# A LayerNorm, sparse-attention and FP8-linear kernel: the banded product as four 32-row strips, with b2, the quantised x and the order of four engines redone

## The reference

```
xn  = layernorm(x)                                   # x: 4096 rows x 1024, f32
A   = (w1 @ w2.T) * sparse_mask                      # 1024 x 1024, non-zero near the diagonal only
y   = gelu(xn @ A + b2)
xq  = fp8_e5m2(xn * x_scale), x_scale = 57344 / max|xn| over all rows
wq  = fp8_e4m3(weight * w_scale)
out = x + y + (xq @ wq.T) / x_scale / w_scale + bias
```

## Time and profile before

| | us |
|---|---|
| median of 3 runs (293.49 to 294.21) | 294.0 |
| the profiled execution | 293.77 |
| its span, first to last instruction | 292.0 |
| PE busy | 251.1 (86%) |
| DVE busy | 208.8 (72%) |
| POOL busy | 205.7 (70%) |
| ACT busy | 203.0 (70%) |

### The profile page before, as it was taken

One profiled execution on the slowest core, in us unless ns is written; L12 is line 12 of the kernel. 1 busy time (PEld: TensorE's weight loads), 2 busy tenths in 40 slices (PEclk: granted clock), 3 DMA queues, 4 the chain that ended last, 5 costly groups with the idle time before them and its releaser, 6 DMA issues.

```text
span 292.0 us, 4911 instructions
## 1 busy us (share of the span) xinstructions
PE 251.1 (86%) x1818; PEld 175.2 (60%) x1818; DVE 208.8 (72%) x225; ACT 203.0 (70%) x239; POOL 205.7 (70%) x137
## 2 busy tenths in 40 slices
PE   0039699990279799999999999999999999999994
PEld 0039688880278366666666656666666666666661
DVE  3888999999997457956659575567746766656563
ACT  1079979999996698676676749667588687772210
POOL 2000499999997189996978786887789897776333
PEclk9999999997559999999999999999999999999999
DMA  6999999999999239999999999999999989879913
GB/s 235 415 411 410 409 407 410 407 384 408 313 226 142 45 69 198 227 216 224 220 216 229 232 192 251 224 226 215 216 240 209 215 222 214 213 203 225 202 72 147
DMA packets 99721, 72.56 MB, mean 249 GB/s; under 512 B 85488, under 2 KB 87280, under 8 KB 99696
## 3 DMA queue, kind: packets, MB, share of 16 engines
q1 hardware_dynamic: 99696, 72.24, 91.2%
HBM read 34.60 MB, written 16.78 MB: 176 GB/s over the span
## 4 chain that ended last, share of the span: by engine, by line
PE 43%; DMA 21%; ACT 10%; SPq 8%; POOL 7%; issue 6%; DVE 4%; ACTq 0%; POOLq 0%; DVEq 0%
PE psF L1054 12%; PE psT L1054 11%; DMA x_all<-in_L_attn_x_dram 8%; PE psY L1037 8%; PE psZ L1037 8%; DMA home<-home 8%; DMA x_all<-in_L_attn_w_dram 4%; POOL x_all L532 3%; SPq L362 3%; POOL home L494 2%; ACT squares L567 2%; PE psT L970 2%; ACT xq L670 2%; PE psY L980 2%; ACT junk L554 2%
## 5 line engine op out<-in xcount | busy, mean ns | idle before, releaser
L532 POOL TENSOR_TENSOR x_all<-x_all,biases 128x1024 f32<-128x1024 f32 x32 | 75.5, 2361 | 35.0 <-DVE x_all L894 35.0
L494 POOL TENSOR_TENSOR home<-home 128x1024 f16<-128x1024 f32 x32 | 68.3, 2133 | 8.6 <-ACT home L663 8.0
L1054 PE MATMUL psT<-wqT,wq_nat 128*128 128x512 f16 x256 | 57.9, 379 | 1.4 <-ACT wq_nat L677 1.4
L1054 PE MATMUL psF<-wqT,wq_nat 128*128 128x512 f16 x256 | 57.9, 379 | 0.0
L663 ACT ACTIVATE home<-home 128x1024 f16<-128x1024 f32 x28 | 29.6, 1057 | 40.3 <-DMA home<-home 40.2
L894 DVE TENSOR_TENSOR x_all<-psZ,x_all 128x1024 f32<-128x1024 f32 x16 | 19.6, 1225 | 36.1 <-ACT psZ L682 36.1
L1037 PE MATMUL psY<-split,home 128*128 128x197 f16 (+2 forms) x480 | 44.2, 249 | 0.1
L1037 PE MATMUL psZ<-split,home 128*128 128x197 f16 (+2 forms) x480 | 44.2, 249 | 0.0
L1037 PEld LDWEIGHTS psY<-split,home 128*128 128x128 f16 x480 | 38.4, 97 | 7.4 <-DMA home<-home 0.6
L1037 PEld LDWEIGHTS psZ<-split,home 128*128 128x128 f16 x480 | 38.4, 97 | 7.1 <-DMA home<-home 0.3
L1054 PEld LDWEIGHTS psT<-wqT,wq_nat 128*128 128x128 fp8e5 x256 | 24.7, 98 | 28.5 <-issue 1.8
(11 more groups left out here) (96 smaller groups left out, 316.7 us busy)
## 6 DMA issues: line engine op xcount, KB each, us to landing
x_all<-in_L_attn_x_dram SPq DMA_DIRECT2D x32, 512.0 KB, 14.5
out_dram<-x_all SPq DMA_DIRECT2D x31, 512.0 KB, 3.3
x_all<-in_L_attn_w_dram SPq DMA_DIRECT2D x16, 512.0 KB, 15.2
x_all<-in_L_ffn_weight_dram SPq DMA_DIRECT2D x8, 512.0 KB, 7.6
squares<-_L_attn_sparse_mask_dram SPq DMA_DIRECT2D x2, 413.5 KB, 3.7
biases<-_L_attn_sparse_mask_dram SPq DMA_DIRECT2D x6, 133.0 KB, 10.5
squares<-_L_attn_sparse_mask_dram SPq DMA_DIRECT2D x2, 349.5 KB, 3.7
squares<-_L_attn_sparse_mask_dram SPq DMA_DIRECT2D x2, 285.5 KB, 3.4
```

Source lines behind the costliest of these rows:

```text
L494: nc.gpsimd.tensor_tensor(hl[:, q % 2, D:2 * D], xs[:, q % 2, :], hl[:, q % 2, 0:D], ALU.subtract).then_inc(xl_ready, 1)
L532: nc.gpsimd.tensor_tensor(x_all[:, SLOT[q], :], x_all[:, SLOT[q], :], bias_bc, ALU.add)\
L1054: ins = nc.tensor.matmul(ps_f[q % 2][:, HALF * h:HALF * h + HALF], quantised(q % XQ_RING)[:, k // 2, k % 2, :], wqT[:, k, HALF * h:HALF * ...
```

## The change

- **Strips.** The 128 contraction rows of each block become four strips of 32 rows, each a matmul at its own `tile_position`, so that four strips can be in the array at once. Each strip takes only the columns that its 32 rows reach (`reach`: 168 instead of 266 in the middle). Different strips write different PSUM banks at any time: `TURNS` lists for each of the six banks (three tiles, two halves) which strip has it in which of 12 steps, and a strip waits for the strip that had the bank before (`strip_done`). Tiles go in groups of three, the first group is tiles 0 and 1.
- **b2** is added for tiles 4 to 31 by one more matmul in each half, of three rows of ones with b2 split in three bf16 rows (`spread_b2`, made once on DVE, for which psT is used); Gelu takes the scale. For tiles 0 to 3 `add_b2` stays.
- **Quantised x.** The normalised x of tiles 4 to 31 carries x_scale already. After the transpose of its parts DVE adds high and low into fp8 (`quantise`); the quantising on ACT and the second transpose by DMA go. Tiles 1 to 3 are summed on DVE (`sum_parts`) and scaled on ACT.
- **fp8 half.** psF alone takes the quantised product, half by half (`add_product`, twice 512 columns); psT becomes the third tile of `ps_y`.
- **bias** is added before the products, on DVE for every third tile from 4 on.
- The orders of PE, DVE, ACT, POOL and SP are rewritten, the rings are 3 and 6 tiles (parts, transposed parts), the last two tiles' row sums go from PE to ACT and DVE, and the mask outside the narrower strips is counted too, as a ninth block, of small transfers.

```diff
-REACH = 32 * (STRIPES - 1) + WINDOW - 1
+REACH = 32 * (STRIPES - 1) + WINDOW - 2
...
+def reach(b, r):
+    row = P * b + SROWS * r
+    return 0 if b == 0 else row - REACH, D if b == KB - 1 else row + SROWS + REACH
...
+GROUPS = range(2, NT, 3)
...
-KIND = "AVPPVVAVVAAVAAVVAAVAVA" + "AAAAAAAA" + "PP"
+KIND = "AVPPVVAVVAAVAAVVAAVAVA" + "AAAAAAAA" + "AV"
...
-WQ_RING, SQ_RING, XQ_RING, HLT_RING = 4, 3, 4, 4
+WQ_RING, SQ_RING, XQ_RING, HL_RING, HLT_RING = 4, 3, 4, 3, 6
...
+TURNS = {2: ("00332211", "11003322", "22110033", "33221100"),
+         3: ("00.33.22.11.", "3.00.11.22.3", ".33.00.11.22", "22.11.00.33.", "1.22.33.00.1",
+             ".11.22.33.00")}
...
+def bias_on_vector(q):
+    return q >= FIRST and q % 3 == 1
...
-        ps_f = (psT, psF)
+        ps_y = (psY, psZ, psT)
+        b2_rest = psT
...
                 if q >= HLT_RING:
-                    sp.wait_ge(y_done, q - HLT_RING + 1)
-                sp.dma_start(hlT[:, q % HLT_RING, :].rearrange("p (k r) -> p k r", r=P), hl[:, q % 2, :],
+                    t = q - HLT_RING
+                    sp.wait_ge(gelu_ready, t + 1)
+                    if t >= FIRST:
+                        wait_xq(sp, t)
+                    elif t > 0:
+                        sp.wait_ge(xT_ready, t)
+                elif q >= 4:
+                    sp.wait_ge(row_max, NT)
...
+                sp.wait_ge(f_added, 2 * q + 2)
+                sp.wait_ge(u_ready, q + 1)
...
+                if b > 0:
+                    sp.wait_ge(mask_counted, b)
                 else:
-                    sp.wait_ge(mask_counted, b)
-                if C0[b] > 0:
-                    sp.dma_start(mask_buf[:, 0:C0[b]], mask_rows[b, :, 0:C0[b]]).then_inc(mask_loaded, 16)
-                if C1[b] < D:
-                    sp.dma_start(mask_buf[:, C0[b]:C0[b] + D - C1[b]], mask_rows[b, :, C1[b]:D])\
-                        .then_inc(mask_loaded, 16)
+                    sp.wait_ge(b2_ready, 1)
...
+            transpose_parts(4)
+            load_mask(0)
+            store(0)
+            transpose_parts(5)
+            load_mask(1)
+            store(1)
+            transpose_parts(6)
+            load_mask(2)
+            transpose_parts(7)
+            for n, q in enumerate(GROUPS):
+                if q + 3 < NT:
+                    store(q)
+                    store(q + 1)
+                    if q + 6 < NT:
+                        transpose_parts(q + 6)
+                    store(q + 2)
+                    for t in range(q + 7, min(q + 9, NT)):
+                        transpose_parts(t)
+                    if n + 3 <= KB:
+                        load_mask(n + 3)
...
+            def add_bias(q):
+                pool.wait_ge(biases_loaded, 32)
+                wait_xs(pool, q)
+                nc.gpsimd.tensor_tensor(x_all[:, SLOT[q], :], x_all[:, SLOT[q], :], bias_bc, ALU.add)\
+                    .then_inc(bias_added, 1)
...
+            quantiser(0)
+            quantiser(1)
+            add_bias(1)
+            later_low(4)
+            add_bias(2)
+            later_low(5)
+            add_bias(3)
+            deviations(2)
+            quantiser(2)
+            later_low(6)
+            later_low(7)
+            add_bias(5)
+            add_bias(6)
+            for q in GROUPS:
+                if q == 5:
+                    deviations(3)
+                    quantiser(3)
+                for t in range(q + 6, min(q + 9, NT)):
+                    later_low(t)
+                    if not bias_on_vector(t):
+                        add_bias(t)
...
+            quantise(0)
             quantise(1)
+            normalise(4)
+            high(4)
+            quantise(2)
+            normalise(5)
+            high(5)
             gelu(0)
+            quantise(3)
+            gelu(1)
+            normalise(6)
+            high(6)
+            normalise(7)
+            high(7)
+            for q in GROUPS:
+                for t in range(q, q + 3):
+                    gelu(t)
+                for t in range(q + 6, min(q + 9, NT)):
+                    normalise(t)
+                    high(t)
...
+            def sum_parts(q):
+                wait_hlT(dve, q)
...
+                nc.vector.tensor_tensor(xT, hlT[q][:, 0:D], hlT[q][:, D:2 * D], ALU.add).then_inc(xT_ready, 1)
...
+            def spread_b2():
+                dve.wait_ge(row_max, NT)
+                then(nc.vector.tensor_scalar(b2_part, b2_bc, b2_mul, not_first[:, :], ALU.mult, ALU.mult))
+                then(nc.vector.scalar_tensor_tensor(out=b2_rest[:, :], in0=b2_bc, scalar=b2_mul, in1=b2_part,
+                                                    op0=ALU.mult, op1=ALU.add))
+                then(nc.vector.tensor_scalar(b2_part, b2_rest[:, :], third[:, :], None, ALU.mult))
+                nc.vector.tensor_tensor(b2_rows, b2_rest[:, :], b2_part, ALU.add).then_inc(b2_ready, 1)
+
+            def quantise(q):
+                wait_hlT(dve, q)
+                dve.wait_ge(f_done, 2 * (q - XQ_RING) + 2)
+                nc.vector.tensor_tensor(quantised(q % XQ_RING), hlT[q % HLT_RING][:, 0:D],
+                                        hlT[q % HLT_RING][:, D:2 * D], ALU.add, saturate=False)\
+                    .then_inc(xq_ready, 1)
...
+                dve.wait_ge(f_done, 2 * q + h + 1)
+                if q == NT - 1 or (q, h) == (NT - 2, 1):
+                    dve.wait_ge(u_ready, q + 1)
+                else:
+                    wait_bias(dve, q)
+                nc.vector.scalar_tensor_tensor(out=x_q, in0=psF[:, cols], scalar=f_mul, in1=x_q,
+                                               op0=ALU.mult, op1=ALU.add).then_inc(f_added, 1)
...
+            sum_parts(1)
+            nc.vector.tensor_scalar(f_mul, x_inv, inv_ws, 1.0 / XSCALE, ALU.mult, ALU.mult)
+            nc.vector.tensor_scalar(y_mul, a_inv, x_inv, 1.0 / XSCALE, ALU.mult, ALU.mult).then_inc(y_scale, 1)
+            dve.wait_ge(x_scale, 1)
+            then(nc.vector.tensor_scalar(b2_mul, a_mul, x_mul, XSCALE, ALU.mult, ALU.mult))
+            add_product(0, 0)
+            sum_parts(2)
+            add_product(0, 1)
+            add_b2(1)
+            add_product(1, 0)
+            sum_parts(3)
+            add_product(1, 1)
+            spread_b2()
+            add_product(2, 0)
             add_gelu(0)
+            add_product(2, 1)
+            add_gelu(1)
+            add_product(3, 0)
+            count_mask(0)
+            quantise(4)
+            add_product(3, 1)
+            count_mask(1)
+            add_bias(4)
+            quantise(5)
+            count_mask(2)
+            quantise(6)
+            for n, q in enumerate(GROUPS):
+                if q < FIRST:
+                    add_b2(q)
                     add_b2(q + 1)
+                if q + 3 < NT:
+                    add_product(q + 2, 0)
+                    add_gelu(q)
+                    add_product(q + 2, 1)
                     add_gelu(q + 1)
+                    add_product(q + 3, 0)
...
+                    add_gelu(q + 2)
+                    add_product(q + 3, 1)
+                    if q + 5 < NT - 1:
+                        add_product(q + 4, 0)
+                    if q + 5 < NT:
+                        quantise(q + 5)
+                        add_bias(q + 5)
+                    if q + 5 < NT - 1:
+                        add_product(q + 4, 1)
+                    if n + 3 <= KB:
+                        count_mask(n + 3)
+                    for t in range(q + 6, min(q + 8, NT)):
+                        quantise(t)
+                if n + 3 == KB:
+                    dve.wait_ge(mask_counted, KB + 1)
                     nc.vector.tensor_reduce(off_cnt, cnt[:, :], AX_X, ALU.add).then_inc(off_ready, 1)
+            add_gelu(NT - 3)
+            add_product(NT - 2, 0)
+            add_gelu(NT - 2)
+            add_product(NT - 2, 1)
+            add_gelu(NT - 1)
+            add_product(NT - 1, 0)
+            add_product(NT - 1, 1)
...
+                for q in group:
+                    if q >= FIRST:
+                        pe.wait_ge(b2_ready, 1)
+                    wait_hlT(pe, q)
+                    if q >= 3:
+                        pe.wait_ge(u_ready, q - 2)
...
+                while min(step) < steps:
+                    r = min(filter(can_go_on, range(NS)), key=lambda r: spent[r])
...
+                    if begins and strip_before(r, n):
+                        before, m = strip_before(r, n)
+                        pe.wait_ge(strip_done[before], base + m + 1)
...
+                                           tile_position=(SROWS * r, 0))
+                    spent[r] += hi - lo + 8
+                    if not todo[r]:
+                        ins.then_inc(strip_done[r], 1)
+                        step[r] += 1
+                        todo[r] = pieces(r, step[r]) if step[r] < steps else []
...
+            def ffn(q):
+                wait_xq(pe, q)
                 for h in range(2):
+                    if q >= 1:
```

(41 more changed lines are left out.)

365 lines of the change are left out of this document (196 added, 169 removed).

## The result

The changed kernel takes 363.8 us (median of 358.8 to 372.7) against 294.1 before: ratio 1.227, interval 1.216 to 1.239. I had forecast 288 and faster. The profiled execution has a span of 360.7 us too. The first `ffn` starts at 98.94, and attention(5..7) at 146.2, the upper end of what I had written down. From there to the end of the span it is 214.5 us where I had summed 143.0: the 72 us are lost in the steady loop.

What follows compares the result with a forecast made beforehand. PE alone was taken to bound the loop, 6.05 us a tile. Start-up 143.6, seven groups 114.1, last two groups 24.8, DVE and store 4.1, around the span 1.8: 288.4 us, forecast 288 (own range 282 to 293; 8 in 10 within 277 to 301).

Steps and rivals of the forecast that it cites:

- x_scale at 97.4, first `ffn` at 98.7: Before the loop: x_scale and the first `ffn` keep their old times; late row sums cost 0 (bounds 0 and +1.2 us).
- The port: In the loop, DVE operations with two SBUF inputs and POOL's exclude each other: 16.0 us of port time per 15.86 us group.
- 16.3 us for DVE's group: Length of a three-tile loop group with about half the port waits, between 15.86 and 17.5 us; seven groups 114.1 us.
- P = 115.5 (112.7 to 118.4): Start-up: time when product (2, 0), for which ffn(3) waits, ends on DVE; 112.7 without port waits, 118.4 with them.
- attention(5..7) at 143.6 (139.4 to 146.5): End of start-up: the banded product of tiles 5 to 7 starts at 143.6 us, after P, 26.7 us and 1.4 us.
- the 6.8 us wait ahead of `ffn(5)`: Start-up: PE waits 6.8 us for DVE's add_product(4, 0), late behind mask counts and other DVE work.
- Attention on PE: 5.5 us for three: Loop: four strips streaming at once take 1.84 us a tile against 2.60, 23 us less PE work over 30 tiles.
- rival 4: Strips don't go together: pairs start 0.025 to 0.031 us apart, 2.9 to 3.6 us a tile, 314 to 333 us; chance 0.14.
- my 286.6: Forecast span: start-up to 143.6, seven groups 114.1, last two groups 24.8, DVE and store 4.1 us.
- Mask counts "0.9 us in 5 of the 7 groups": DVE's list in the loop: a mask count adds 0.9 us in 5 of 7 full groups, 13.0 us a group in all.
- DMA, ACT, SP hidden: Loop: DMA needs about 5.1 us a tile against 5.3 or more available, ACT loses 1.23 a tile; nothing waits.
- The clock, 1.4 us lost once: Start-up: after PE's gaps the clock falls, costing 1.4 us before attention(5..7).

Runs made afterwards that it cites:

- experiment 4: The probe: kernel before, with four blocks of matmuls (strips and full rows) that wait for nothing put ahead of PE's work; 128 pairs every 3.45 to 6.2 us.
- experiment 5: Changed kernel with only the mask load moved to the front of SP's list for the group: 335.4 us, ratio 1.147.
- experiment 9: Changed kernel with two strips of 64 rows, mask load moved to the front, and start-up reordered (`spread_b2` behind tile 2's products): 304.2 us, ratio 1.038.
- experiment 8: Kernel before with its attention as two strips of 64 rows, one tile at a time, nothing else changed: 295.6 us, ratio 1.008.

## Why the prediction was wrong

- *x_scale at 97.4, first `ffn` at 98.7.* Right: 98.94.
- *The port.* Right in kind: operations on both engines stretch to up to 3.4 us. My 16.3 us for DVE's group stands beside 16.6 measured, but only as busy time of DVE: in no complete kernel did it become the group's length, which was 17.6 us in the best and 21.3 to 30.9 in the changed kernel's full groups.
- *P = 115.5 (112.7 to 118.4).* The upper end: product (2, 0) ends at 117.7, `spread_b2` took 7.8 us (1.95, 3.27, 1.28, 1.23), and PE waited 7.0 us ahead of ffn(3), not about 3.
- *attention(5..7) at 143.6 (139.4 to 146.5).* 146.2, in the range, but the parts were wrong: the 6.8 us wait ahead of `ffn(5)` was 0.5, because attention(2..4) took 12.0 us and covered it.
- ***Attention on PE: 5.5 us for three.*** **The first step that failed.** Four strips do stream together: the probe has 14.0 ns a pair at the full clock (159 pairs in 2.19 us), so rival 4 as I put it (pairs 25 to 31 ns apart) is refuted. What I left out is where 116 pairs a tile come from: PE's instructions arrive in lines of 128 pairs, one per 3.5 to 6.2 us, and fewer than two lines are at hand. 348 pairs in 5.5 us need three lines where the supply gives one. Measured 9.0 to 12.0 us. This is the larger part of what the sum lacks: with the mask wait out of the way (experiment 5) the span is 44.8 us over my 286.6, and 39.2 of that are the nine attentions from attention(5..7) on, 88.7 us where I had 9 x 5.5. The rival's price, 2.9 to 3.6 us a tile, and its 314 to 333 us were nearly right for a wrong reason (mask moved: 335). The old kernel's 46 pairs in 6.05 us never came near that limit, so its trace could not show it; its page had 15 fetches against the 36 that the count of the new instructions gives, and I did not count them.
- ***Mask counts "0.9 us in 5 of the 7 groups".*** **The second.** I priced the operation and not the wait ahead of it (and there are six counts in these groups, not five), though I had walked exactly this wait for the blocks 1 and 2. In the loop it is the same chain: load issued behind a transpose that waits for `low`, count ahead of two quantisations. 51.9 us of DVE's time between 150 and 340, and 26.5 us of the kernel's.
- *DMA, ACT, SP hidden.* Transfers yes (share 0.51 to 0.86 in the stretches between 140 and 340); SP's order, as said, no.
- *The clock, 1.4 us lost once.* It was lost again and again, behind holes of PE: 48 matmuls of `ffn` took 11.9 us instead of 10.4 behind the strips' holes (from 210.50, granted clock 0.89), 32 took 9.1 instead of 6.9 behind the mask wait (0.77).

The account, in the order in which the causes were removed, from the medians: mask load moved 360.7 to 334.2, 26.5; four strips to two 24.8, to 309.4; start-up order 5.2, to 304.2; the bias with its port waits 9.1, to 295.1. Together 65.6 of 66.6. That the steps nearly fill the difference doesn't prove the split: the last one leaves out a bias that the kernel before adds, and two strips are a change of their own. The order matters: with the mask still late, two strips gave only 12.1, because the strips' holes partly lay in front of the mask wait. So the largest share is shown to be two causes of about equal size that cover each other. That the port waits, and not the bias's own time, are the most of the last 9.1 is argued from the durations; it wasn't tried apart. No version beat the kernel before: the best complete one is experiment 9, 11 us slower; a group of its loop without a wait is 0.6 us shorter, and its start-up loses more. Why the supply period is longer beside busy DMA queues stays open; experiment 4 shows that it is, and that the fetch starts later, not that it lasts longer.

## What to carry to other kernels

Before splitting matmuls into strips, count instructions as well as columns, and count them over the dense stretch and not over the whole loop: set the time of 128 pairs there against the period of the instruction fetches under the kernel's own DMA load (3.7 to 4.6 us). Four strips ran 128 pairs in 2.2 us and stood, two strips took 4.8 us for 128 and did not. Over the whole group four strips have 396 pairs, 3.1 lines, which would have seemed to fit: too little is stored ahead while `ffn` runs. When a wait is moved onto a queue or an engine's list, walk it once for the steady loop and not just for the start: what is behind it, and what the thing waited for is itself queued behind. A load that no one needs soon belongs ahead of transfers that wait, and a block of other work put between strips must neither be waited for by itself nor delay what others wait for.

## What the runs showed of the hardware

- PE's instructions come in lines of 128 pairs. Once a line is used up faster than the next comes, PE stands with no releaser in the trace; period 3.45 to 3.73 us beside idle DMA queues, 3.7 to 4.6 in this kernel's loop, 6.2 beside saturated ones. Fewer than two lines are at hand (118 to 234 pairs before the first hole of a group).
- Strips of 32 rows: 14.0 ns a pair with 128 columns at 2.4 GHz, 26 ns at 1.2 GHz; 8.1 ns with 32 columns at 1.2 GHz. Full rows with 32 columns: 25.0 ns a pair at 2.4 GHz, 26.7 at 1.2.
- Between a full-row matmul and strips each change costs about 0.1 us (0.1 to 0.16 ahead of the odd one, 0.1 behind it); a handover of a bank between strips by semaphore 0.35 us from start to start, with one tile at a time (experiment 8).
- Two-input SBUF operations of DVE and GpSimd, overlapping, both record the wait in their duration (3.36 and 3.38 for 2.36 and 1.22), so it isn't seen as idle time: look for means over the shortest of the same form.
